# Spread sums of attention by two matmuls with ones, and two banks for keys, in a two-layer hybrid kernel on one Trainium2 core

## The chip, the cores and the metric

The kernel runs on one core of a Trainium2 chip (trn2). The metric is the time of one execution on the device in microseconds (us), lower is better. Before the change three runs gave a median of 2713.94 us, 2713.19 to 2719.81.

## What is computed

All data is float32. The input x is (4, 128, 64, 64): 4 batches of 4096 tokens with 128 channels. Two layers follow one another.

```python
# layer 0: group norm, full softmax attention over 4096 tokens of a batch
h = group_norm(x, norm_w, norm_b)            # 32 groups
q, k, v = h @ Wq + bq, h @ Wk + bk, h @ Wv + bv
attn = softmax(q @ k.T * C ** -0.5)          # 4096 x 4096 for each batch
x = x + (attn @ v) @ Wo + bo
# layer 1, on tokens t = (4, 4096, 128)
kv = silu(norm(t) @ W_kv.T)                  # 8 heads, k and v of 128 each
s = q_proj . k;  e = exp(s - cummax(s))
t = t + mean over heads of cumsum(e * v) / cumsum(e)
p = softmax(norm(t) @ router_w + router_b)   # 8 experts, the 2 best kept
t = t + sum over the 2 best of p_e * (norm(t) @ expert_w[e] + expert_b[e])
```

## The kernel before

Every engine has its own program, written out by hand; semaphores tie them together, and each engine runs strictly in the order written. Names below are those of the code, L numbers are lines of the profiled kernel.

**First stage** (`softmax_attention`). A block is 512 queries of a batch: 4 batches of 8 blocks, 32 blocks, numbered n (i = n % 8 inside its batch). A block meets its batch's 4096 keys in 32 tiles of 128 keys; g counts the 1024 tiles and t = g % 32. In the turn of tile g, PE (TensorE) issues three score matmuls (L374 to L376, high and low parts of keys and queries), one matmul that looks for row maxima a block ahead (L359), and three that weigh the values of tile g - 3 (L388 to L390). ACT takes the exponential (`exps`, L500) and its rounded high part (`high`, L505), POOL (GpSimd) the low part (`low`, L224), DVE (VectorE) the row maximum (`row_max`, L638) and the running sum of exponentials (`add`, L654). The rings of tiles are 4 deep, the banks of scores and of maxima 2 deep.

The sum left in `den` (128 keys-within-tile x 512 queries) still has to be added over partitions. `denominators(n)` does that on PE in turn `den_slot`, 1 or 2 of the next block, into the bank `pj_ps`; DVE takes the reciprocal a turn later (`inverse`, L663), SP sends it through DRAM and back as rows spread over all partitions, and `finish` (L671, L675) uses it in turn 10. The single bank `pj_ps` also serves the projections of queries (`project_q`, L278, turn 21 or 22), keys (`project_k`, L294, turns 3, 7, ... of block i = 6) and values (`project_v`, L311, turns 8, 12, ... of block i = 7 and turns 0 and 4 of the next block) of the next batch.

```python
for i in range(QT):                                                     # L405
    mm = pe.matmul(pj_ps[:, i:i + 1], den[:, i * C:(i + 1) * C], ones[:, 0:1], start=True, stop=True)
```

**Second stage** (`scan_attention_and_experts`). The unit is 512 tokens of one batch, 32 of them. In step j the kernel works on the keys of unit k = j, the values of unit v = j - 5 and the experts of unit f = j - 11, so that a step holds three units at once for j from 11 to 31; 43 steps in all. Each step has 8 slots h, one for each head. In slot h PE issues the value matmuls of head h (`value`, three, L1143 to L1145), its key matmuls (`key`, three), and one product of an expert (`expert`, L1186), whose 8 products are added in the bank `mo_ps` after a bias (`expert_bias`, L1178). ACT applies Silu to both; DVE multiplies by the weight (`weigh`, L1373) and scans (`scan`, L1381); POOL multiplies tokens by the gate of an expert (`gated`, L1049) and adds up the heads (`add_head`, L1061). DVE adds the experts to the tokens (`output`, L1401) and the heads (`residual`, L1388). `G_LAG`, `X_LAG` say in which slot the first gate product and the first expert product of a unit stand. Four steps make a group (4 batches of the same 512 tokens): step j % 4 = 0 has the scans and the reciprocal of the weights (L1345 to L1366) on DVE, step 1 the router's logits (L1124, L1126), step 2 the choice of the two experts on DVE (L1423 to L1467).

PSUM has 8 banks. The second stage gives three to values (`v_ps`), one to keys (`k_ps`; for j < 5 a bank of values serves as a second one), one each to row sums and to statistics, and two to expert sums (`mo_ps`). In unit 26 and later, half of the gate products are made by DVE (`by_vector`, `FREE` = 26).

## Time and profile before

| | |
|---|---|
| median of 3 runs | 2713.94 us |
| the profiled execution, its own time | 2719.66 us |
| its span, first to last instruction | 2717.9 us |
| PE busy | 2553.1 us (94%) |
| DVE, ACT, POOL busy | 2152.6 (79%), 1840.3 (68%), 2058.7 us (76%) |
| granted TensorE clock, mean | 0.983 |
| DMA engines, mean in the second stage | about 0.5 to 0.6 busy |

The first stage ends near 1831 us, the second takes the rest. A matmul's duration in the records is longer than its turn on the array, since matmuls overlap; the spacing of starts is what counts. A float32 matmul (experts, projections) is recorded as two instructions and a float32r one as one. Idle time of an engine that nobody waits for costs nothing.

### The profile page before, as it was taken

The page shows a single profiled execution, that of the slowest core. Times are in us where ns is not written, and L with a number is a line of the kernel's source. Part 1 is how long each engine was busy: PE and PEld are TensorE (multiplying, and loading weights), DVE is VectorE, ACT ScalarE, POOL GpSimd, SP SyncE. Part 2 cuts the span into 40 slices and gives each one's busy share as a digit, 9 for nine tenths or more (in the row PEclk, how much of TensorE's full clock was granted, in tenths as well). Part 3 has the DMA queues.
Part 4 walks back from the last instruction along what each step waited for, and adds up shares of the span by engine and source line. Part 5 has one row for each costly group of instructions (what it writes and reads, how often), then busy time and mean ns, then how long its engine had stood idle before and what let it go on. Part 6 is the DMA issues. An engine that isn't in the chain of part 4 may idle for free. (4 is left out here: it accounts for less than half of the span.)

```text
span 2717.9 us, 37024 instructions
## 1 busy us (share of the span) xinstructions
PE 2553.1 (94%) x10851; PEld 1856.2 (68%) x10851; DVE 2152.6 (79%) x3225; ACT 1840.3 (68%) x3375; POOL 2058.7 (76%) x1688
## 2 busy tenths in 40 slices
PE   6999999999999999999999999997889999999868
PEld 4888877788887788887778888773545555555433
DVE  6788887788887778888778978852888988888884
ACT  5667677676667766677766766765877777767540
POOL 4777777777776777777677777772558988989994
PEclk9999999999999999999999999998999999999899
DMA  1000000100000010000001000101445565555545
GB/s 66 9 9 9 13 12 9 40 8 13 12 9 9 8 41 15 9 9 12 9 13 32 9 12 13 47 8 53 171 172 218 186 240 214 213 204 196 227 173 198
DMA packets 58105, 198.38 MB, mean 73 GB/s; under 512 B 12752, under 2 KB 15376, under 8 KB 40496
## 3 DMA queue, kind: packets, MB, share of 16 engines
q1 hardware_dynamic: 57904, 196.03, 20.4%
q8 instruction: 86, 1.41, 0.2%
q14 instruction: 115, 0.94, 0.1%
HBM read 178.04 MB, written 17.96 MB: 72 GB/s over the span
## 5 line engine op out<-in xcount | busy, mean ns | idle before, releaser
L224 POOL TENSOR_TENSOR p_lo<-pf,p_hi 128x512 fp32r<-128x512 f32 x1024 | 1320.0, 1292 | 434.2 <-ACT p_hi L505 431.7
L500 ACT ACTIVATE pf<-s_ps 128x512 f32<-128x512 f32 x1024 | 612.8, 598 | 530.4 <-PE s_ps L376 529.3
L638 DVE TENSOR_REDUCE mx<-m_ps 128x1 f32<-128x512 f32 x1024 | 702.2, 687 | 296.1 <-PE m_ps L359 292.2
L654 DVE TENSOR_TENSOR sum_ps<-sum_ps,pf 128x512 f32<-128x512 f32 x960 | 661.6, 689 | 21.1 <-ACT pf L500 20.8
L505 ACT CAST p_hi<-pf 128x512 fp32r<-128x512 f32 x1024 | 627.2, 613 | 0.0
L374 PE MATMUL s_ps<-q_hi,kd_hi 128*128 128x512 f32 x1024 | 427.2, 417 | 0.0
L359 PE MATMUL m_ps<-w_both,q_hi 128*128 128x512 f32 x1024 | 403.6, 395 | 7.0 <-DVE mx L638 6.0
L388 PE MATMUL om_ps<-p_hi,v_hi 128*128 128x512 f32 x1024 | 401.3, 392 | 4.6 <-POOL p_lo L224 4.6
L376 PE MATMUL s_ps<-q_lo,kd_hi 128*128 128x512 f32 x1024 | 399.7, 390 | 0.0
L375 PE MATMUL s_ps<-q_hi,kd_lo 128*128 128x512 f32 x1024 | 399.6, 390 | 0.0
L389 PE MATMUL om_ps<-p_hi,v_lo 128*128 128x512 f32 x1024 | 399.1, 390 | 0.0
L390 PE MATMUL om_ps<-p_lo,v_hi 128*128 128x512 f32 x1024 | 398.8, 389 | 0.0
L1049 POOL TENSOR_TENSOR xg<-gate_b,tv 128x512 f32<-128x512 f32 x232 | 303.8, 1316 | 46.0 <-PE mo_ps L1186 31.9
L1061 POOL TENSOR_TENSOR acc<-acc,ay 128x512 f32<-128x512 f32 x192 | 255.2, 1329 | 61.6 <-DVE ay L1381 56.6
L1186 PE MATMUL mo_ps<-xg,ew 128*128 128x512 f32 x512 | 271.1, 625 | 28.1 <-POOL xg L1049 25.6
L1381 DVE TENSOR_TENSOR_SCAN ay<-ay,carry,v_ps 128x512 f32<-128x512 f32 x224 | 286.7, 1280 | 8.7 <-DVE v_ps L1373 0.3
L1250 ACT ACTIVATE v_ps<-v_ps 128x512 f32<-128x512 f32 x256 | 149.7, 585 | 166.1 <-PE v_ps L1145 164.6
L1373 DVE TENSOR_TENSOR v_ps<-bq,v_ps 128x512 f32<-128x512 f32 x256 | 174.9, 683 | 85.4 <-ACT v_ps L1250 70.2
L359 PEld LDWEIGHTS m_ps<-w_both,q_hi 128*128 128x128 f32 x1024 | 192.4, 188 | 60.1 <-DVE mx L638 17.2
L388 PEld LDWEIGHTS om_ps<-p_hi,v_hi 128*128 128x128 f32 x1024 | 192.1, 188 | 55.5 <-POOL p_lo L224 14.2
L374 PEld LDWEIGHTS s_ps<-q_hi,kd_hi 128*128 128x128 f32 x1024 | 192.7, 188 | 50.5 <-issue 15.1
L375 PEld LDWEIGHTS s_ps<-q_hi,kd_lo 128*128 128x128 f32 x1024 | 192.7, 188 | 48.5 <-issue 12.7
(205 smaller groups left out, 3481.0 us busy)
## 6 DMA issues: line engine op xcount, KB each, us to landing
bq<-weight_rows SPq DMA_DIRECT2D x64, 1024.0 KB, 6.3
gate_b<-gate_rows SPq DMA_DIRECT2D x64, 1024.0 KB, 4.8
xb<-in_x_dram SPq DMA_DIRECT2D x8, 1024.0 KB, 6.2
rb_sb<-inverse_rows SPq DMA_DIRECT2D x32, 256.0 KB, 3.9
tokens<-xb SPq DMA_DIRECT2D x32, 256.0 KB, 2.0
tp<-tokens SPq DMA_DIRECT2D x32, 256.0 KB, 5.4
rb<-norm_rows SPq DMA_DIRECT2D x32, 256.0 KB, 5.4
tv<-tokens SPq DMA_DIRECT2D x32, 256.0 KB, 5.5
```

What stands on the lines that cost most here:

```text
L224: nc.gpsimd.tensor_tensor(p_lo[:, r, :], pf[:, r, :], p_hi[:, r, :].bitcast(F32), ALU.subtract).then_inc(lo_done, 1)
L359: pe.matmul(m_ps[:, j % 2, :], q_hi[:, n % QRING, sub * C:(sub + 1) * C], kp[:, chunk * BANK:(chunk + 1) * BANK], start=True, stop=True).t ...
L374: pe.matmul(dst, kd_hi[:, ks], q_hi[:, q, :], start=False, stop=False, skip_group_check=True)
L375: pe.matmul(dst, kd_lo[:, ks], q_hi[:, q, :], start=False, stop=False, skip_group_check=True)
L376: pe.matmul(dst, kd_hi[:, ks], q_lo[:, q, :], start=False, stop=True, skip_group_check=True).then_inc(s_pe, 1)
L388: pe.matmul(o, v_hi[:, t, :], p_hi[:, r, :], start=(t == 0), stop=False)
L389: pe.matmul(o, v_lo[:, t, :], p_hi[:, r, :], start=False, stop=False)
L390: pe.matmul(o, v_hi[:, t, :], p_lo[:, r, :], start=False, stop=(t == KT - 1)).then_inc(pv_pe, 1)
L500: nc.scalar.activation(pf[:, g % RING, :], s_ps[:, g % 2, :], ACT.Exp, scale=SCALE).then_inc(exp_done, 1)
L505: nc.scalar.copy(p_hi[:, g % RING, :], pf[:, g % RING, :]).then_inc(hi_done, 1)
L638: nc.vector.tensor_reduce(mx[:, n % 2, sub, chunk:chunk + 1], m_ps[:, j % 2, :], AX.X, ALU.max).then_inc(m_max, 1)
L654: nc.vector.tensor_tensor(sum_ps[:], sum_ps[:], p, ALU.add).then_inc(sum_done, 1)
```

## The change

First stage:

- `denominators` of all blocks but the last adds `den` over partitions by two float32r matmuls of 512 columns, with a matrix of ones as the stationary operand and the high and the low part of `den` as moving ones, so that every row of `pj_ps` holds all 512 sums. ACT makes the high part (`high_den`, turn 2), POOL the low part (`low_den`, turn 3); PE's turn is now 5 (6 where i = 0).
- `inverse` (turn 6 or 7) has to bring the sums to partitions: DVE multiplies the bank by the identity, four blocks wide, into `den`, sums each block of 128 (`tensor_reduce`) and takes the reciprocal of the 128 x 4 result.
- What waited for `inv_done` before using `pj_ps` waits for `den_held`, the first of these three. `finish` moves from turn 10 to 14, and the one-time work of blocks 27 and 30 moves a few turns.

Second stage:

- Keys have two banks in all steps, alternating by head; expert sums have one. From unit 27 on, odd units take a bank of values, which are done by then.
- `add_head` of head h moves from slot h + 1 to h + 2, `gated` and `expert` one slot later (`G_LAG` 4, `X_LAG` 6), except that the eighth product of a unit shares the seventh's slot; `output` moves from slot 5 to 4, `residual` from 1 to 2. `logits` moves from slot 3 to 5, what follows it accordingly.
- `expert_bias` of a unit up to 26 waits for `output` of the unit before.

```diff
-        def den_slot(i):
-            return 1 if i == NB - 2 else 2
+        def den_slot(n):
+            return 6 if n % NB == 0 else 5
...
@@ -223,6 +224,10 @@
                 r = g % RING
                 nc.gpsimd.tensor_tensor(p_lo[:, r, :], pf[:, r, :], p_hi[:, r, :].bitcast(F32), ALU.subtract).then_inc(lo_done, 1)
...
+            def low_den(n):
+                pool.wait_ge(den_h, n + 1)
+                nc.gpsimd.tensor_tensor(den_lo[:], den[:], den_hi[:].bitcast(F32), ALU.subtract).then_inc(den_l, 1)
...
             for g in range(TILES + 1):
                 if g >= 1:
                     low(g - 1)
+                if KT <= g < TILES and g % KT == 3:
+                    low_den(g // KT - 1)
...
             def denominators(n):
-                pe.wait_ge(sum_done, (n + 1) * KT)
                 pe.wait_ge(q_l, min(n + 3, BLOCKS))
                 if n % NB == NB - 1 and n + 1 < BLOCKS:
-                    pe.wait_ge(v_l, (n // NB + 1) * CK + 7)
+                    pe.wait_ge(v_l, (n // NB + 2) * CK)
+                elif n % NB == NB - 3 and n // NB + 1 < B:
+                    pe.wait_ge(k_diff, (n // NB + 1) * CK + 1)
                 elif n % NB == NB - 2 and n // NB + 1 < B:
                     pe.wait_ge(k_diff, (n // NB + 2) * CK)
-                after(pe, inv_done, n)
+                after(pe, den_held, n)
                 if n == BLOCKS - 1:
                     pe.wait_ge(wt_lo, 4)
                 if n == L_AT:
                     pe.wait_ge(diff_dve, 1)
-                for i in range(QT):
-                    mm = pe.matmul(pj_ps[:, i:i + 1], den[:, i * C:(i + 1) * C], ones[:, 0:1], start=True, stop=True)
-                mm.then_inc(den_pe, 1)
+                if n < BLOCKS - 1:
+                    pe.wait_ge(den_l, n + 1)
+                    pe.matmul(pj_ps[:], ones_r[:], den_hi[:], start=True, stop=False)
+                    pe.matmul(pj_ps[:], ones_r[:], den_lo[:], start=False, stop=True).then_inc(den_pe, 1)
+                else:
+                    pe.wait_ge(sum_done, (n + 1) * KT)
+                    for i in range(QT):
+                        mm = pe.matmul(pj_ps[:, i:i + 1], den[:, i * C:(i + 1) * C], ones[:, 0:1], start=True, stop=True)
+                    mm.then_inc(den_pe, 1)
...
+            def high_den(n):
+                act.wait_ge(sum_done, (n + 1) * KT)
+                after(act, den_pe, n)
+                nc.scalar.copy(den_hi[:], den[:]).then_inc(den_h, 1)
...
+                    if n and t == 2:
+                        high_den(n - 1)
...
-                    after(dve, den_pe, n)
+                    after(dve, diag_sum, n)
                     nc.vector.tensor_tensor(den[:], sum_ps[:], p, ALU.add).then_inc(sum_done, 1)
 
             def inverse(n):
                 dve.wait_ge(den_pe, n + 1)
                 after(dve, inv_out, 16 * (n - 1))
-                nc.vector.reciprocal(rinv[:, n % 2, :], pj_ps[:, 0:QT]).then_inc(inv_done, 1)
+                if n == BLOCKS - 1:
+                    nc.vector.reciprocal(rinv[:, n % 2, :], pj_ps[:, 0:QT]).then_inc(inv_done, 1)
+                    return
+                blocks = den[:].rearrange("p (i c) -> p i c", i=QT)
+                nc.vector.tensor_tensor(blocks, pj_ps[:].rearrange("p (i c) -> p i c", i=QT),
+                                        ident[:].unsqueeze(1).to_broadcast([C, QT, C]), ALU.mult).then_inc(den_held, 1)
+                dve.wait_ge(den_held, n + 1)
+                nc.vector.tensor_reduce(dsum[:], blocks, AX.X, ALU.add).then_inc(diag_sum, 1)
+                dve.wait_ge(diag_sum, n + 1)
+                nc.vector.reciprocal(rinv[:, n % 2, :], dsum[:]).then_inc(inv_done, 1)
...
-                    if n and t == den_slot(i) + 1:
+                    if n and t == den_slot(n) + 1:
                         inverse(n - 1)
-                    if n and t == 10:
+                    if n and t == 14:
...
-    V_LAG, F_LAG, G_LAG, X_LAG = 5, 11, 3, 5
+    V_LAG, F_LAG, G_LAG, X_LAG, A_LAG = 5, 11, 4, 6, 2
...
         v_ps = psum("v_ps", [C, 3, BANK])
-        k_ps = psum("k_ps", [C, BANK])
+        k_ps = psum("k_ps", [C, 2, BANK])
         row_ps = psum("row_ps", [C, BANK])
-        mo_ps = psum("mo_ps", [C, 2, BANK])
+        mo_ps = psum("mo_ps", [C, BANK])
         st_ps = psum("st_ps", [C, BANK])
...
-        def two_banks(k):
-            return k < V_LAG
...
         def value_bank(v, h):
             return v_ps[:, (v * HEADS + h) % 3, :]
 
         def key_bank(k, h):
-            return v_ps[:, 1, :] if two_banks(k) and h % 2 else k_ps[:]
+            return k_ps[:, h % 2, :]
+
+        def sum_bank(f):
+            return v_ps[:, 0, :] if f > FREE and f % 2 else mo_ps[:]
+
+        def expert_slot(e):
+            return X_LAG + min(e, E - 2)
...
-                    if h == 0 and stage(v - 1):
-                        add_head(v - 1, HEADS - 1)
+                    if h < A_LAG and stage(v - 1):
+                        add_head(v - 1, HEADS + h - A_LAG)
...
-                    if stage(v) and h:
-                        add_head(v, h - 1)
+                    if stage(v) and h >= A_LAG:
+                        add_head(v, h - A_LAG)
...
             def key(k, h):
                 if h == 0:
                     pe.wait_ge(xl_pool, k + 1)
-                after(pe, k_act, k * HEADS + h - (1 if two_banks(k) else 0))
+                after(pe, k_act, k * HEADS + h - 1)
                 project(key_bank(k, h), h, 0, k).then_inc(k_pe, 1)
 
             def value(v, h):
-                if v == 0 and h == 0:
-                    pe.wait_ge(k_act, V_LAG * HEADS)
                 after(pe, y_dve, v * HEADS + h - 2)
                 project(value_bank(v, h), h, 1, v).then_inc(v_pe, 1)
...
             def expert_bias(f):
                 s, b, cols = place(f)
-                after(pe, out_dve, f - 1)
+                if f > FREE and f % 2:
+                    pe.wait_ge(y_dve, NBLK * HEADS)
+                after(pe, out_dve, f - 1 if f > FREE else f)
                 pe.wait_ge(gt_act, s + 1)
-                pe.matmul(mo_ps[:, f % 2, :], eb_hi[:, b, :], gt[:], start=True, stop=False)
-                pe.matmul(mo_ps[:, f % 2, :], eb_lo[:, b, :], gt[:], start=False, stop=False)
+                pe.matmul(sum_bank(f), eb_hi[:, b, :], gt[:], start=True, stop=False)
+                pe.matmul(sum_bank(f), eb_lo[:, b, :], gt[:], start=False, stop=False)
...
-                    if norm2_at(j, 1) is not None and h == 3:
+                    if norm2_at(j, 1) is not None and h == 5:
                         logits(norm2_at(j, 1))
-                    if norm2_at(j, 1) is not None and h == 5:
+                    if norm2_at(j, 1) is not None and h == 6:
                         turn_logits(norm2_at(j, 1))
-                    if stage(f - 1) and h < X_LAG:
-                        expert(f - 1, E + h - X_LAG)
-                    if stage(f) and h >= X_LAG:
-                        if h == X_LAG:
-                            expert_bias(f)
-                        expert(f, h - X_LAG)
+                    if stage(f) and h == X_LAG:
+                        expert_bias(f)
+                    for e in range(E):
+                        if stage(f) and expert_slot(e) == h:
+                            expert(f, e)
+                        if stage(f - 1) and expert_slot(e) == h + HEADS:
+                            expert(f - 1, e)
...
-                    if stage(f - 1) and h == X_LAG:
+                    if stage(f - 1) and h == expert_slot(E - 1) - HEADS:
                         output(f - 1)
...
-                    if stage(v - 1) and h == 1:
+                    if stage(v - 1) and h == 2:
                         residual(v - 1)
```

**Where rows moved.** DVE, first stage, round `inverse` (L663 before, L686 to L691 now; L638 and L657 are `row_max`, L654 and L673 `add`). Before:

```order
L654 TENSOR_TENSOR sum_ps<-sum_ps,pf 128x512 [waits sum_done,exp_done]
L638 TENSOR_REDUCE mx<-m_ps 128x1 [waits m_pe]
L654 TENSOR_TENSOR sum_ps<-sum_ps,pf 128x512 [waits sum_done,exp_done]
L663 RECIPROCAL rinv<-pj_ps 128x4 [waits inv_out,den_pe]
L638 TENSOR_REDUCE mx<-m_ps 128x1 [waits m_pe]
L654 TENSOR_TENSOR sum_ps<-sum_ps,pf 128x512 [waits sum_done,exp_done]
```

Now:

```order
L673 TENSOR_TENSOR sum_ps<-sum_ps,pf 128x512 [waits sum_done,exp_done]
L657 TENSOR_REDUCE mx<-m_ps 128x1 [waits m_pe]
L673 TENSOR_TENSOR sum_ps<-sum_ps,pf 128x512 [waits sum_done,exp_done]
L686 TENSOR_TENSOR den<-pj_ps,ident 128x512 [waits inv_out,den_pe]
L689 TENSOR_REDUCE dsum<-den 128x4 [waits den_held]
L691 RECIPROCAL rinv<-dsum 128x4 [waits diag_sum]
L657 TENSOR_REDUCE mx<-m_ps 128x1 [waits m_pe]
L673 TENSOR_TENSOR sum_ps<-sum_ps,pf 128x512 [waits sum_done,exp_done]
```

One short instruction has become three, and it stands three tiles later in the block.

PE, second stage, slots 3 and 4 of a step: products of experts into `mo_ps`, values into `v_ps`, keys into `k_ps`. Before:

```order
L1186 MATMUL mo_ps<-xg,ew 128x512 [waits xg_pool]
L1143 MATMUL v_ps<-xh,w_both 128x512 [waits y_dve]
L1144 MATMUL v_ps<-xl,w_both 128x512
L1145 MATMUL v_ps<-xh,w_both 128x512
L1143 MATMUL k_ps<-xh,w_both 128x512 [waits k_act]
L1144 MATMUL k_ps<-xl,w_both 128x512
L1145 MATMUL k_ps<-xh,w_both 128x512
L1186 MATMUL mo_ps<-xg,ew 128x512 [waits xg_pool]
```

Now:

```order
L1217 MATMUL mo_ps<-xg,ew 128x512 [waits xg_pool]
L1174 MATMUL v_ps<-xh,w_both 128x512 [waits y_dve]
L1175 MATMUL v_ps<-xl,w_both 128x512
L1176 MATMUL v_ps<-xh,w_both 128x512
L1174 MATMUL k_ps<-xh,w_both 128x512 [waits k_act]
L1175 MATMUL k_ps<-xl,w_both 128x512
L1176 MATMUL k_ps<-xh,w_both 128x512
L1217 MATMUL mo_ps<-xg,ew 128x512 [waits xg_pool] x2
```

In slot 4 two products stand behind each other, the seventh and the eighth of the unit; the bias of the next unit comes in slot 6, where before it came in slot 5.

DVE, second stage, the same step from slot 2 or 3: `tv<-acc,tv` is `residual`, `tv<-mo_ps,tv` is `output`. Before:

```order
L1373 TENSOR_TENSOR v_ps<-bq,v_ps 128x512 [waits v_act,b_in2]
L1381 SCALAR_TENSOR_TENSOR ay<-ay,carry,v_ps 128x512 [waits y_pool,a_act,z_dve]
L1373 TENSOR_TENSOR v_ps<-bq,v_ps 128x512 [waits v_act,b_in0]
L1381 SCALAR_TENSOR_TENSOR ay<-ay,carry,v_ps 128x512 [waits y_pool,a_act,z_dve]
L1401 TENSOR_TENSOR tv<-mo_ps,tv 128x512 [waits x_pe]
L1373 TENSOR_TENSOR v_ps<-bq,v_ps 128x512 [waits v_act,b_in0]
```

Now:

```order
L1420 SCALAR_TENSOR_TENSOR tv<-acc,tv 128x512 [waits tv_in0,y_pool]
L1405 TENSOR_TENSOR v_ps<-bq,v_ps 128x512 [waits v_act,b_in2]
L1413 SCALAR_TENSOR_TENSOR ay<-ay,carry,v_ps 128x512 [waits y_pool,a_act,z_dve]
L1433 TENSOR_TENSOR tv<-mo_ps,tv 128x512 [waits x_pe]
L1405 TENSOR_TENSOR v_ps<-bq,v_ps 128x512 [waits v_act,b_in0]
L1413 SCALAR_TENSOR_TENSOR ay<-ay,carry,v_ps 128x512 [waits y_pool,a_act,z_dve]
```

`output` stands one head earlier than it did, ahead of the first weighing of the second half of the heads (`b_in0`), and `residual` one head later.

## Rows read from the trace of the kernel before

**Rows 1.** Busy time by stretch (us, count), then clock, DMA share, GB/s.

```profile
60.00:1831.00 1771.00, 1749.07 (x7808) 1417.28 (x7806) 1428.23 (x2305) 1243.01 (x2340) 1344.16 (x1044) 1.00 0.05 15
1831.00:2080.20 249.20, 203.80 (x860) 111.17 (x861) 170.90 (x200) 182.11 (x311) 138.65 (x137) 0.92 0.40 142
2080.20:2471.50 391.30, 361.52 (x1450) 206.78 (x1449) 334.02 (x408) 275.48 (x485) 353.37 (x302) 0.98 0.58 210
```

**Rows 2.** Timeline of PE round one block's denominators: start us, us.

```profile
220.69 0.39 PE L388 MATMUL om_ps<-p_hi,v_hi 128*128 128x512 f32 x1
...
221.37 0.95 PE L405 MATMUL pj_ps<-ones,den 128*128 128x1 f32 x8
222.18 0.48 PE L374 MATMUL s_ps<-q_hi,kd_hi 128*128 128x512 f32 x1
222.50 0.39 PE L375 MATMUL s_ps<-q_hi,kd_lo 128*128 128x512 f32 x1
```

**Rows 3.** Timeline, first stage: the low part of one tile and its use.

```profile
224.34 1.29 POOL L224 TENSOR_TENSOR p_lo<-pf,p_hi 128x512 fp32r<-128x512 f32 x1 [1.20 <-ACT p_hi L505]
...
227.94 0.39 PE L388 MATMUL om_ps<-p_hi,v_hi 128*128 128x512 f32 x1
```

**Rows 4.** Timeline of DVE, first stage: a block's finish, then back on time.

```profile
235.69 1.08 DVE L671 TENSOR_TENSOR om_ps<-om_ps,rb_sb 128x512 f32<-128x512 f32 x1
236.81 0.75 DVE L675 SCALAR_TENSOR_TENSOR xb<-om_ps,bvo,xb 128x512 f32<-128x512 f32 x1
...
245.59 0.69 DVE L638 TENSOR_REDUCE mx<-m_ps 128x1 f32<-128x512 f32 x1 [0.26 <-PE m_ps L359]
```

**Rows 5.** Waits of PE, first stage: us in total, times, longest.

```profile
PE om_ps L388 <- POOL p_lo L224: 4.1, 10, 0.5
PE pj_ps L278 <- DVE kd L624: 2.5, 3, 0.8
...
PE m_ps L359 <- DVE mx L638: 0.7, 2, 0.4
```

**Rows 6.** Waits of PE, 2080.2 to 2471.5 us; last row 1831 to 2080.2.

```profile
PE k_ps L1143 <- ACT sk L1246: 19.4, 12, 2.3
PE st_ps L1124 <- ACT sq L1262: 5.6, 3, 2.0
PE v_ps L1143 <- DVE ay L1381: 2.4, 2, 1.2
PE mo_ps L1186 <- POOL xg L1049: 1.7, 4, 0.4
...
PE k_ps L1143 <- ACT sk L1246: 19.5, 15, 3.5
```

**Rows 7.** Timeline of PE and of ACT round one wait, second stage.

```profile
2296.75 0.39 PE L1145 MATMUL v_ps<-xh,w_both 128*128 128x512 f32 x1
2299.39 0.50 PE L1143 MATMUL k_ps<-xh,w_both 128*128 128x512 f32 x1 [2.25 <-ACT sk L1246]
...
2293.21 1.28 ACT L1317 ACT_TABLE_LOAD   x1
...
2296.35 1.28 ACT L1322 ACT_TABLE_LOAD   x1
...
2298.75 0.59 ACT L1246 ACTIVATE sk<-k_ps 128x512 f32<-128x512 f32 x1
```

**Rows 8.** Timeline of DVE in a step with row sums, second stage.

```profile
2353.48 1.26 DVE L1356 TENSOR_TENSOR_SCAN u_r<-e_r,u_r,zeros 128x512 f32<-128x512 f32 x1
2354.78 3.35 DVE L1362 RECIPROCAL b_r<-u_r 128x512 f32<-128x512 f32 x1
```

**Rows 9.** Timeline of PE after the last values: logits, then their transposes.

```profile
2650.95 1.52 PE L1124 MATMUL st_ps<-tv,rwz 128*32 128x512 f32 x8
...
2653.26 1.98 PE L1186 MATMUL mo_ps<-xg,ew 128*128 128x512 f32 x4
2655.08 0.60 PE L1132 MATMUL st_ps<-ident,l_sb 128*128 128x128 f32 x4
```

More of the change, by code:

```diff
@@ L85, in softmax_attention @@
         nmax = sb("nmax", [C, 2, QT])
-        den = sb("den", [C, QB])
+        den, dsum = sb("den", [C, QB]), sb("dsum", [C, QT])
+        wv, wo, wvT = (den[:, i * C:(i + 1) * C] for i in range(3))
+        den_hi, den_lo = sb("den_hi", [C, QB], F32R), sb("den_lo", [C, QB], F32R)
         rinv = sb("rinv", [C, 2, QT])
@@ L265, in project_q @@
                 else:
-                    after(pe, inv_done, n - 2)
+                    after(pe, den_held, n - 2)
                 if n >= 2 and n % NB == 0:
@@ L327, in center_experts @@
                 if g == 0:
[L328 removed]
+                    pe.wait_ge(den_held, E_AT)
                 else:
@@ L1308, in _ @@
                         square_of_mean(norm1_at(j, 0))
-                    if norm2_at(j, 1) is not None and h in (1, 2):
-                        for b in (2 * h - 2, 2 * h - 1):
+                    if norm2_at(j, 1) is not None and h in (3, 4):
+                        for b in (2 * h - 6, 2 * h - 5):
                             square_out(norm2_at(j, 1), b)
-                    if norm2_at(j, 1) is not None and h == 4:
+                    if norm2_at(j, 1) is not None and h == 5:
                         hold_logits(norm2_at(j, 1))
```

46 lines of the change are left out of this document (21 added, 25 removed).

## The prediction

> **What bounds the kernel now.** I read the busy time by stretch first [rows 1]. In the first stage, 60 to 1831 us, PE is busy 1749.07 of 1771.00 us, DVE 1428, POOL 1344 and ACT 1243: PE sets the time there, and whatever leaves PE's queue leaves the total, as long as nobody makes PE wait. In the second stage, from 2080.2 to 2471.5 us, the work repeats in groups of four steps, four of them in 391.3 us, 97.8 us each. PE's records cover 361.5 us, POOL's 353.4, DVE's 334.0. None is alone the bound: here PE waits, and the question is what for.
>
> The timeline of PE [rows 2] gives prices. Three float32r matmuls take 220.69 to 221.37, so 0.227 us each. The waits of PE in the first stage [rows 5] are small: 4.1 us on POOL's low parts, 2.5 us on a key chunk, 0.7 us on row maxima. In the second stage [rows 6] PE waits 29.1 us in the four groups, 7.3 us each, and 19.4 of them are a key matmul that waits for ACT to empty the single key bank. One such wait is shown [rows 7]: ACT loads a table, works, and loads another, 2293.21 to 2297.6, so the next Silu of a key starts at 2298.75, and PE stands from about 2297.1 to 2299.39. Without waits a group would take PE 97.8 - 7.3 = 90.5 us; POOL's 353.4 / 4 = 88.4 us is close behind, DVE's 83.5 less so.
>
> **First stage, removed and added on PE.** The old denominators are eight records from 221.37; the second matmul behind them, L375, starts at 222.50. Taking off one ordinary spacing, they cost 222.50 - 221.37 - 0.227 = 0.90 us [rows 2]. The new ones are two float32r matmuls of 512 columns, 2 x 0.227 = 0.45 us. 31 blocks change: 31 x 0.45 = **13.9 us less**.
>
> The Trainium skill, page TensorE: Matmul & The Clock Gate, section Back-to-back issue gap, gives a matmul of 1 to 64 columns about 60 cycles, some 25 ns at full clock. By that the eight cost an estimated 0.2 us, and the change would lose 0.25 us a block, 8 us in all. The trace disagrees: their turns are 0.81 / 8 = 0.1 us each (221.37 to 222.18), and the matmul behind them comes late as well. The sum goes by the trace.
>
> **What the other engines get.** ACT gains one copy of 128x512 in a block (nearest: 0.59 us of a Silu, [rows 7]), POOL one subtraction (1.29 us), DVE a multiplication and a reduction. For the cover of POOL: the low part of tile 3 ends at 224.34 + 1.29 = 225.63 and PE wants it at 227.94 [rows 3], 2.3 us later, so 1.29 us of extra work in turn 3 is hidden, and POOL wins back 7 x 0.227 - 1.29 = 0.3 us in every tile. In the block with i = 0 a low part of keys stands one turn ahead, and the two together reach 2.3 us; if this is late, PE waits about 0.5 us as in the ten cases of [rows 5], three times. For DVE: the multiplication reads a bank and the identity and is nearest to a 512-wide operation of 0.69 us or, being four blocks wide, to the 1.08 us of `finish` [rows 4]; the reduction is nearest to the 0.69 us of L638. Together 1.4 to 1.8 us at once. `finish` puts 1.8 us (235.69 to 237.48) on DVE in one go, which waits for PE again at 245.59, and PE waited for row maxima only 0.7 us in the whole stage. So I cost this at nothing; if the cover were gone, the wait that [rows 5] shows, up to 0.4 us, would come in 31 blocks, 12 us. Round trip of the inverses: `inverse` is four turns later and so is `finish`, nothing changes.
>
> **Added waits on `pj_ps`.** In block i = 6 a key chunk now stands two turns before the denominators (3 and 5), and these wait for DVE to finish its difference. The same distance, chunk in turn 19 and query projection in turn 21, costs PE 2.5 us in three batches today [rows 5]; I add 2.5 us. What is queued behind is the whole of PE. The next key chunk, and once the first weight transposes, stand two turns behind the denominators and wait for DVE's multiplication. DVE reaches it about a turn later; between nothing and 1 us at four places, I take 0.3 each, 1.2 us. The value chunks of block i = 0 keep their distance of two turns.
>
> First stage: -13.9 + 2.5 + 1.2 = **-10 us**, bounds -14 (no wait anywhere) and about 0 (the 12 us of DVE added in part).
>
> **Second stage, the second key bank.** In the case of [rows 7] PE would go on with the waiting key matmuls (0.7 us), a product (0.91 us: four records from 2653.26 to 2655.08 are two products [rows 9]) and the next value (0.7 us), until about 2299.4, when the Silu of 2298.75 is done. The wait of 2.25 us goes nearly whole. So most of the 19.4 us could go. But PE then meets the next limit. DVE is the slow one in the steps with row sums, where a scan and a reciprocal stand 1.26 + 3.35 us in its queue [rows 8]; values have three banks only, and POOL's 88.4 us is only 2 us under PE's 90.5. I take half of the 7.3 us as won, a group of 94.1 us. The 20 steps with keys, values and experts together (j = 12 to 31) are five groups: 5 x 3.7 = **-18.5 us**. Bounds: all of it, -37; none, 0. Before that, 1831 to 2080.2, PE waits 19.5 us for ACT [rows 6], but its busy share there is low ([rows 1], 203.80 of 249.2 us) and DVE and the start-up of the pipeline set the pace; I take -3.
>
> **The later slots.** POOL adds heads one slot later, which removes waits of POOL on DVE, and the squares of the logits are asked for later, which should spare part of PE's 5.6 us [rows 6]; both are inside the half. The eighth product now stands one slot behind its gate product where it had two; POOL lags most in the quiet steps, and this is why I don't take more than half. At the end, logits come behind the last two products, where these used to stand between logits and transposes: 1.8 us of products (2653.26 to 2655.08) no longer hide ACT's copy, and the residual waits one gate product longer. Nothing covers this, the end of the kernel hangs on the gates of the last group: **+2.5 us**, between 0 and 5.
>
> Second stage: -18.5 - 3 + 2.5 = **-19 us**. Together -29 us: the profiled execution of 2719.66 would be 2690.7. It is 5.7 us above the median of the runs, 2713.94, and from that the same difference gives **2685 us**.
>
> **Rival 1, the waits only move.** PE's waits in the second stage become waits for values on DVE or for gate products on POOL, since their busy times are within 8% of each other [rows 1]. Against it: the waits of PE on these two are 2.4 and 1.7 us today. Then only the first stage counts: 2713.9 - 10 = 2704.
>
> **Rival 2, the single bank of expert sums makes it slower.** The bias of unit f waits for `output` of f - 1, and `output` now stands before the weighing of head 4 and waits for the eighth product, which is behind a key and another product in PE's queue: some 0.7 + 1.8 us of waiting on DVE in each step, with four weighings and scans queued behind it; in the step with row sums the 4.6 us of [rows 8] stand ahead of `output` too, and PE's bias arrives 1.4 us after scan 3, so it would wait up to 3.9 us. If DVE's loss comes through at 1.5 us a step in 26 steps: +39 - 10, 2743 us. It decides for slower from 0.4 us net a step on (10 / 26). Against it: PE needs the scan of head 4 only for value 7, and has a value, two keys, row sums, bias and product to do meanwhile; today PE waits for DVE only 2.4 us in four groups [rows 6]. The Trainium skill, page Perfetto Trace Analysis, section Matmuls, says that independent matmul groups should rotate through different banks, so that the emptying of one overlaps the next. The change does this for keys and undoes it for expert sums; no row of before shows the single bank.
>
> **Rival 3, the whole gain.** All PE waits of the groups go, and the first stage adds none: -14 - 37 - 3 = 2660 us. For it speaks that ACT's table loads are the cause of most of the waits; against it POOL's 88.4 us.
>
> **Numbers.** Forecast (2670 to 2700) 0.58, rival 1 0.24, rival 3 0.11, rival 2 0.07. The range 2663 to 2707 holds the forecast, rival 1 and half of rival 3. 0.3% is 8.1 us, about what a measurement can tell, so the border is 2705.8: rival 1 lies six parts in ten under it, and a little of it above 2722. Faster 0.83, same 0.09, slower 0.08.
>
> **What the next profile would show.** The end of the first stage near 1821 instead of 1831 us; the spacing round the denominators 0.45 us and an ordinary block 0.45 us shorter; PE waiting for POOL's low parts and for row maxima no more than today; a new wait of denominators on the key difference, near 0.8 us, three times. In the second stage: waits of key matmuls on Silu near zero, a group of steps of about 94 us, PE's waits on values or on POOL grown to 3 us a group. Wrong would be: a group at 97 or more with waits on DVE in PE's list (rival 1), a bias that waits for `output` in most steps (rival 2), or a first stage that has not shrunk because row maxima come late.

## The result, and the profile after

The changed kernel takes 2700.22 us (median of 7 runs, 2697.51 to 2707.79) where the kernel before takes 2718.55 on the same chip. The ratio, formed from the means (2702.11 and 2717.64), is 0.9943, with an interval of 0.9927 to 0.9959: 15.5 us less, of the 29 forecast (the medians differ by 18.3). In all the runs of this document three executions took far longer than the others of their kernel, 2912.7, 4222.4 and 7775.6 us, and the ratios leave them out. The profiled execution took 2707.49 us with a span of 2705.7, against 2719.66 and 2717.9: 12.2 us less. By place:

| stretch of the span | before | after | difference | forecast |
|---|---|---|---|---|
| to the last denominators | 1830.60 | 1825.29 | -5.3 | -10 |
| from there to the last residual | 816.48 | 803.44 | -13.0 | -21.5 |
| from there to the last output | 67.5 | 73.6 | +6.1 | +2.5 |

Busy time by stretch, changed kernel (columns as in [rows 1]):

```profile
60.00:1826.00 1766.00, 1741.50 (x7639) 1401.37 (x7637) 1462.30 (x2369) 1259.08 (x2372) 1382.21 (x1077) 1.00 0.05 15
1826.00:2075.90 249.90, 202.82 (x867) 114.93 (x866) 172.47 (x203) 181.49 (x315) 139.22 (x137) 0.91 0.39 142
2075.90:2460.50 384.60, 356.80 (x1453) 205.63 (x1452) 338.63 (x407) 274.18 (x485) 355.50 (x304) 1.00 0.57 215
```

Four groups of steps, counted from the residual that opens the first, now take 384.6 us instead of 391.3, 96.2 each instead of 97.8; 94.1 were forecast. VectorE is busy 4.6 us longer in a stretch 6.7 us shorter, though it does the same work. Waits of PE in these four groups, after:

```profile
PE v_ps L1174 <- DVE ay L1413: 11.6, 15, 1.2
PE mo_ps L1209 <- DVE tv L1433: 9.2, 4, 3.0
PE st_ps L1169 <- DVE g L1499: 7.0, 4, 1.8
```

The key's wait for its Silu, 19.4 us in [rows 6], is gone, and the list is nearly as long as before: 27.8 us, all of it on VectorE, where before it was 29.6 (the 29.1 of the prediction and 0.5 at the gates). L1209 is the bias product into the single bank of expert sums, L1169 the turn of the gates. The chain of waits of the changed kernel says what stands behind the bias wait (start, length, place):

```profile
2244.97 2.35 DVE u_r L1388
...
2247.52 3.10 issue
2250.62 0.64 DVE tv L1433
...
2251.30 0.50 PE mo_ps L1209
2251.80 0.23 PE mo_ps L1210
2252.03 1.31 PE mo_ps L1217 x2
```

The 3.10 us called issue are the reciprocal, which holds VectorE's queue. So PE waits for `output`, which stands behind the sums and reciprocal of the rows. This recurs at 2148.59, 2244.97, 2342.22 and 2438.61, once a group. And the sums have become slower: 2.33 us, where [rows 8] show 1.26. The timeline of POOL and DVE shows what goes with it. Changed kernel:

```profile
2244.94 1.30 POOL L1092 TENSOR_TENSOR acc<-acc,ay 128x512 f32<-128x512 f32 x1
2246.19 2.22 POOL L1080 TENSOR_TENSOR xg<-gate_b,tv 128x512 f32<-128x512 f32 x1
...
2244.97 2.34 DVE L1388 TENSOR_TENSOR_SCAN u_r<-e_r,u_r,zeros 128x512 f32<-128x512 f32 x1
2247.35 3.35 DVE L1394 RECIPROCAL b_r<-u_r 128x512 f32<-128x512 f32 x1
```

Kernel before, POOL beside the scan of [rows 8]:

```profile
2353.54 2.29 POOL L1061 TENSOR_TENSOR acc<-acc,ay 128x512 f32<-128x512 f32 x1
```

Before, the scan starts 0.06 us ahead of POOL's addition: the scan takes 1.26 us and the addition 2.29 instead of 1.28. Now the addition starts 0.03 us ahead, the scan takes 2.34, and the gate product behind the addition takes 2.22 instead of 1.28. It is so in all four groups of either trace. The Trainium skill, page SBUF — State Buffer, section Who interferes with whom, says that a VectorE instruction with two SBUF inputs contends with a GpSimd instruction that reads SBUF, that the ports which the two engines share are an exclusive lock, and that the order of issue decides who blocks. These traces agree.

The lags of the change are not needed for this, and the added microsecond need not be its price. The kernel that has the change in its first stage alone runs the second stage of before, instruction for instruction, and shows:

```profile
2247.54 2.42 DVE L1384 TENSOR_TENSOR_SCAN u_r<-e_r,u_r,zeros 128x512 f32<-128x512 f32 x1
2247.61 1.27 POOL L1089 TENSOR_TENSOR acc<-acc,ay 128x512 f32<-128x512 f32 x1
2248.84 2.20 POOL L1077 TENSOR_TENSOR xg<-gate_b,tv 128x512 f32<-128x512 f32 x1
```

Its scan takes 2.38 to 2.42 us in all four groups, although the record of the scan starts up to 0.07 us ahead of the addition's, so starts so close together in the records don't tell who comes first. And its groups take 97.85 us, where the kernel before, with scans of 1.26, has 97.8. In that order of instructions, where PE doesn't wait for `output` at the bias, the longer scan cost nothing that can be seen. What it costs in the changed kernel no run isolates.

A small instruction of the gates' chain grows too. Before, then after (shortest, median, longest, ns):

```profile
L1449 DVE TENSOR_TENSOR gap<-top x4: 148/149/150, 2112.6 to 2407.8; 128x16 f32<-128x16 f32 x4
```

```profile
L1481 DVE TENSOR_TENSOR gap<-top x4: 1259/1267/1269, 2102.7 to 2392.7; 128x16 f32<-128x16 f32 x4
```

The timeline shows what stands beside it in the changed kernel:

```profile
2102.14 0.67 DVE L1420 SCALAR_TENSOR_TENSOR tv<-acc,tv 128x512 f32<-128x512 f32 x1
2102.30 1.66 POOL L1092 TENSOR_TENSOR acc<-acc,ay 128x512 f32<-128x512 f32 x1 [1.23 <-DVE ay L1413]
2102.72 1.27 DVE L1481 TENSOR_TENSOR gap<-top 128x16 f32<-128x16 f32 x1
```

`residual`, which the change put in this slot, now stands between the scan and this subtraction, so that POOL's addition, which waits for the same scan, starts 0.42 us ahead of the subtraction. Before, the subtraction came right behind the scan and 0.16 us ahead of the addition (2112.64 and 2112.80). With the second stage of before it takes 0.15 us in every group; in every run with this `residual` it takes 1.2 us or more in these groups. It stands ahead of `g`, for which PE waits 7.0 us in four groups at L1169 (0.5 before).

In the first stage, PE round the new denominators, then its waits (60 to 1826 us):

```profile
227.43 0.39 PE L395 MATMUL om_ps<-p_lo,v_hi 128*128 128x512 f32 x1
227.66 0.46 PE L412 MATMUL pj_ps<-den_hi,ones_r 128*128 128x512 f32 x1
227.96 0.40 PE L413 MATMUL pj_ps<-den_lo,ones_r 128*128 128x512 f32 x1
228.19 0.40 PE L379 MATMUL s_ps<-q_hi,kd_hi 128*128 128x512 f32 x1
```

```profile
PE om_ps L393 <- POOL p_lo L225: 5.6, 13, 0.5
...
PE pj_ps L285 <- DVE kd L643: 2.6, 3, 0.9
PE pj_ps L412 <- issue: 2.4, 3, 0.8
...
PE m_ps L364 <- DVE mx L657: 1.3, 3, 0.5
PE pj_ps L412 <- POOL den_lo L229: 0.4, 1, 0.4
```

The two new matmuls take 228.19 - 227.66 = 0.53 us, not 0.45: the first has a spacing of 0.30. An ordinary block fell from 53.09 to 52.73 us, by 0.36. The trace calls the releaser of three waits at L412 `issue`; in the code they are for the key difference (DVE's L643, which ends 0.11 us before the matmul at 389.79).

### The profile page after: what moved, and what is told of

The parts are those of the page before. It is cut to its first block and busy times, and to the rows that moved or that the text cites. A ratio compares the mean times of both kernels' runs of the same rounds, so it can differ in the third digit from the quotient of the medians.

```text
span 2705.7 us, 36807 instructions
## 1 busy us (share of the span) xinstructions
PE 2539.7 (94%) x10665; PEld 1841.5 (68%) x10665; DVE 2194.0 (81%) x3287; ACT 1851.4 (68%) x3406; POOL 2095.1 (77%) x1719
## 5 line engine op out<-in xcount | busy, mean ns | idle before, releaser
L657 DVE TENSOR_REDUCE mx<-m_ps 128x1 f32<-128x512 f32 x1024 | 701.0, 686 | 256.7 <-PE m_ps L364 249.8
L673 DVE TENSOR_TENSOR sum_ps<-sum_ps,pf 128x512 f32<-128x512 f32 x960 | 661.5, 689 | 20.0 <-ACT pf L512 19.5
L1217 PE MATMUL mo_ps<-xg,ew 128*128 128x512 f32 x464 | 242.9, 622 | 20.8 <-POOL xg L1080 18.0
```

The costliest lines, as they stand in the source:

```text
L657: nc.vector.tensor_reduce(mx[:, n % 2, sub, chunk:chunk + 1], m_ps[:, j % 2, :], AX.X, ALU.max).then_inc(m_max, 1)
L673: nc.vector.tensor_tensor(sum_ps[:], sum_ps[:], p, ALU.add).then_inc(sum_done, 1)
```

## The experiments

Ratios are against the kernel before, from 5 rounds each (3 for the single wait); the changed kernel has 0.9943. A difference of 0.001 is 2.7 us, and an interval is about 0.0013 wide to either side.

**The stages apart.** One kernel has the change in the first stage alone, one in the second alone.

> The change's first stage with the second stage of before. Theory (the first stage gave about 7 us, the body of the second about 13, and the tail took 6 back): 6 to 8 us under before, ratio near 0.9972; ordinary blocks of 52.73 us. Rival (the first stage's own term of 10 us holds and the profile of the change had a slow start): 10 us, ratio 0.9963. Second rival (the first stage gave nothing in the total, as its end is hidden by the start of the second): ratio 1.000.

> The change's second stage with the first stage of before. Theory: 7 to 9 us under before (13 from the steps, 6 lost after the last value), ratio near 0.997; the groups of four steps 96.2 us against 97.8. Rival (the two parts don't add, the second stage alone gives the whole 15): ratio 0.9943.

Measured: 0.9973 (0.9960 to 0.9985) and 0.9979 (0.9970 to 0.9988), some 7.3 and 5.7 us. Together 13, near the 15.5: within the noise the parts add. The groups take 97.85 and 96.4 us.

**The banks back**, with the lags kept.

```diff
-        k_ps = psum("k_ps", [C, 2, BANK])
-        mo_ps = psum("mo_ps", [C, BANK])
+        k_ps = psum("k_ps", [C, BANK])
+        mo_ps = psum("mo_ps", [C, 2, BANK])
```

> The changed kernel with one bank for keys and two for expert sums, as before, all its later slots kept. Theory (the second key bank pays 4 to 5 us a group in waits on Silu, and the single sum bank costs 2.3 us a group back): key waits on Silu return at some 19 us in four groups, the bias no longer waits for output, groups of 98 to 99 us, and the total is 8 to 12 us over the change. Rival (the gain of the second stage is from the later slots of POOL, not from the banks): groups stay at 96.2 us or fall to 94, total equal or lower than the change.

Measured: 0.9989 (0.9980 to 0.9997), groups of 98.1 us: the theory. The wait of keys is back, that of the bias gone:

```profile
PE k_ps L1174 <- ACT sk L1278: 21.5, 11, 2.3
```

With the lags in place the banks are worth 0.0046, 12 us. Against the first stage alone (0.9973) the lags without the banks cost 0.0016, 4 us, which the intervals don't separate from nothing.

**The burst of sums and reciprocal, moved.** One head later, and one head earlier (with ACT's exponential):

```diff
-                        if h == 3:
+                        if h == 4:
                             sums(s)
                             inverse(s)
-                        if h == 4:
+                        if h == 5:
                             new_weights(s)
```

> The changed kernel with the row sums' scan and reciprocal one slot later on DVE (slot 4 instead of 3, behind output and the scan of head 4), and the new weights one slot later. Theory (PE's bias waits for output because 4.6 us of scan and reciprocal stand ahead of it, 2.3 us in each group): the wait of mo_ps L1209 on output goes from 9.2 us in four groups to under 1, groups of about 94 us, 10 to 15 us less in all. Rival (DVE is the bound in that step and the wait only moves to PE's value matmuls): PE's waits on scans grow by the same 2 us a group and the total stays within 3 us. A third case: the weights' rows go out about 2 us later and ACT and DVE wait longer for bq, slower by a few us.

> The second-stage softmax of the gates one head earlier: ScalarE's exponential of the rows at h = 1, VectorE's sums and reciprocal at h = 2, its new weights at h = 3 (in the changed kernel 2, 3 and 4). Theory A (the gain of the second stage was given back at the chain reciprocal, new weights, row DMA, next group's gate products): the wait of the bias product on the output (9.2 us in four) and the waits for the landed rows (ScalarE 13.9 us in four, VectorE 6.1) fall to under 3 us together, a group of four steps takes 94 us instead of 96.2, and the time is 8 to 12 us under the changed kernel's. Theory B (VectorE's own work is the bound once the Silu wait is gone, so the reciprocal costs its time wherever it stands): the same waits come back as waits of the value products on VectorE, the groups stay within 0.5 us of 96, and the time within 2 us.

Measured: 0.9986 (0.9977 to 0.9995) and 0.9977 (0.9966 to 0.9989), both slower than where it stands. Later, the weights' rows land late: in the groups ACT waits 18.1 us for them and DVE 10.1 (13.9 and 6.1 in the changed kernel), and PE 20.3 for the values. Earlier, the bias wait is gone and PE stands at a value (one such row, then the sum in the groups):

```profile
2256.68 0.50 PE L1174 MATMUL v_ps<-xh,w_both 128*128 128x512 f32 x1 [3.52 <-DVE ay L1413]
```

```profile
PE v_ps L1174 <- DVE ay L1413: 24.7, 16, 3.5
```

Groups of 97.8 us on average. Neither theory of the second run holds in full: the waits moved, as B says, but grew, from 27.8 to 31.7 us. No wait of ACT or DVE for the weights' rows is left in the trace's list, and the groups are longer all the same, so the late rows are not what holds them up.

**The output ahead of the burst.**

```diff
-                    if stage(f - 1) and h == expert_slot(E - 1) - HEADS:
+                    if stage(f - 1) and h == expert_slot(E - 1) - HEADS and rows_at(j) is None:
                         output(f - 1)
...
                         if h == 3:
+                            if stage(f - 1):
+                                output(f - 1)
                             sums(s)
```

> In the steps with a softmax of the rows, VectorE writes the output of the expert sums at the end of h = 3, ahead of the sums and the reciprocal, instead of at h = 4 behind them. Theory A (TensorE's wait at the bias product, 9.2 us in four, is the price of the single bank of expert sums whose reader stands behind the 5 to 6 us of sums and reciprocal): the wait goes to near zero, a group of four steps falls from about 96.2 to about 94, the time 8 to 12 us under the changed kernel's. Theory B (the burst costs TensorE its time wherever it stands, as in the run with the softmax one head earlier, where the wait came back at the value products): the bias wait goes, the waits of the value products rise by as much, time within 2 us.

Measured: 0.9947 (0.9935 to 0.9959), no change; groups of 95.7 us. The bias wait of 9.2 us is gone and the values' has grown by 7.9, from 11.6. Theory B:

```profile
PE v_ps L1174 <- DVE ay L1413: 19.5, 16, 3.1
```

**Three quarters of the reciprocal left out.** Leaves out 384 of 512 columns of the reciprocal, in all groups but the first.

```diff
-                nc.vector.reciprocal(b_r[:], u_r[:]).then_inc(ri_dve, 1)
+                n = C if s else TOK
+                nc.vector.reciprocal(b_r[:, :n], u_r[:, :n]).then_inc(ri_dve, 1)
```

> Leaves out three quarters of the reciprocal of the rows' sums (128 of 512 columns, in all groups but the first), so that VectorE's burst of sums and reciprocal falls from 5.7 to about 3.2 us. Theory A (this burst is what TensorE waits for, in whatever wait it shows): the bias wait falls from 9.2 us in four to under 1, the wait for landed rows on ScalarE (13.9) and VectorE (6.1) by 2 us a group, groups from 96.2 to about 94, the time 10 us or more under the changed kernel's. Theory B (TensorE's waits are spread over all of VectorE's and GpSimd's work): the bias wait goes and half of it or more comes back at the value products, the time under 4 us less.

Measured: 0.9893 (0.9879 to 0.9906), 13.6 us under the changed kernel. Theory A. The instruction fell by 2.40 us, and the bias wait is all but gone:

```profile
L1395 DVE RECIPROCAL b_r<-u_r x4: 953/954/954, 2141.4 to 2423.6; 128x128 f32<-128x128 f32 x4
```

```profile
PE mo_ps L1209 <- DVE tv L1434: 0.6, 1, 0.6
```

Seven times 2.40 is 16.8; groups took 93.5 us on average instead of 96.2. The reciprocal is on the path of the changed kernel with its whole length, although VectorE is busy only 88% of the stretch. That the scan beside it counts in the same way is likely, but no run shows it.

**The reciprocal in two halves**, 256 columns at h = 3 and 256 at the end of h = 4.

```diff
-                            inverse(s)
+                            inverse(s, 0)
                         if h == 4:
+                            inverse(s, 1)
                             new_weights(s)
```

> The reciprocal of the rows' sums in two halves of 256 columns: the first behind the sums at h = 3, the second at the end of h = 4 ahead of the new weights, so that VectorE's work stays and its burst falls from 5.7 to about 4 us; the output at h = 4 stands behind half a reciprocal only. Theory A (it costs as a burst, since VectorE is idle 28 us in 385 beside it waiting for ScalarE): half of what the quarter reciprocal gave, groups about 95, the time 4 to 8 us under the changed kernel's. Theory B (it costs as total work, VectorE being what the values wait for all through the group): groups stay at 96, time within 2 us.

Measured: 0.9952 (0.9938 to 0.9966), no gain, theory B. The halves take 1.74 us each, 0.13 more in all, and PE waits 19.4 us for values and 2.9 at the bias. The groups take 97.0 us. So VectorE's work in the row steps counts, not the length of one burst.

**The gates turned one head later.**

```diff
-                    if norm2_at(j, 2) is not None and h == 6:
+                    if norm2_at(j, 2) is not None and h == (7 if norm2_at(j, 2) < SUPERS - 1 else 6):
                         turn_gates(norm2_at(j, 2))
...
```

> The turn of the gate rows (the small transposing products and the hold of their result) at h = 7 instead of 6, in all groups but the last. In the changed kernel TensorE waits there 7.0 us in four for VectorE's last gate factor. Theory A (this wait is on the path): it goes to near zero, a group is about 1.5 us shorter, the time 5 to 9 us under the changed kernel's. Theory B (TensorE would wait for the values or for the output right after it anyway): the wait goes and the value waits rise by as much, time within 2 us.

Measured: 0.9924 (0.9911 to 0.9936), 5 us less than the changed kernel, though the two intervals overlap; groups of 94.9 us. The wait of 7.0 us is gone, 4.7 us came back at the values, and 2.6 left the bias. The scan of the row sums fell from 2.33 to 1.80 us as well, so the 5 us are not those of the gates' wait alone.

```profile
PE v_ps L1174 <- DVE ay L1413: 16.3, 22, 1.2
...
PE mo_ps L1209 <- DVE tv L1433: 6.6, 4, 2.4
```

**The lags.** Additions with no lag, with one head of lag, and products one head earlier:

```diff
-    V_LAG, F_LAG, G_LAG, X_LAG, A_LAG = 5, 11, 4, 6, 2
+    V_LAG, F_LAG, G_LAG, X_LAG, A_LAG = 5, 11, 4, 6, 0
```

> Of the change's three lags only GpSimd's additions go back: each head is added in its own step of the loop (A_LAG 0 instead of 2); banks, products and experts stay as changed. Theory A (the later additions are what frees GpSimd from waiting for VectorE's scans, so that the gate products come in time): GpSimd waits for the scans again, TensorE waits for the gate products, groups of four steps take 98 or more, the time 8 to 12 us over the changed kernel's, though the tail is some 2 us shorter. Theory B (GpSimd is busy 92% of the stage and only its order changes): groups stay at 96, and the time is 1 to 3 us less by the shorter tail.

> GpSimd's additions one head behind the scans (A_LAG 1), as in the kernel before, all else as changed. Theory A (the second head of lag matters: the last two products share a slot, and their gate products must not stand behind an addition that waits for VectorE): TensorE waits for the gate products some 5 us in four groups, groups 97 to 98, the time 3 to 8 us over the changed kernel's. Theory B (one head of lag was enough): groups stay at 96, the stretch after the last residual 1 to 2 us shorter, the time the same or up to 2 us less.

> Only the lags of the gate products and of the experts go back (G_LAG 3 and X_LAG 5 instead of 4 and 6); two key banks, one bank of expert sums and the later additions stay. The output then stands at h = 3, ahead of sums and reciprocal. Theory A (the place of the output against the reciprocal decides): the bias wait of 9.2 us in four goes, groups about 94, time 6 to 12 us under the changed kernel's. Theory B (with the additions two heads later, products one head earlier come too early for GpSimd and for the residual two heads behind): TensorE waits for the gate products, 3 us a group or more, groups 97 or more, time over the changed kernel's.

The first was misnamed: the kernel before adds one head behind, so 0 goes one step past it. It takes 1.0144 (1.0129 to 1.0158), 55 us over the changed kernel, far more than either theory said: POOL waits 47.7 us in the groups for a scan with a gate product queued behind, and PE for that product:

```profile
PE mo_ps L1217 <- POOL xg L1080: 34.0, 27, 3.1
```

With one head of lag the time is that of the changed kernel, 0.9945 (0.9932 to 0.9957), theory B, with groups of 95.1 us. In them 4.8 us of waits for gate products have come, and the bias wait has fallen from 9.2 to 1.6. The earlier products give 0.9957 (0.9945 to 0.9969) and groups of 96.3 us: the bias wait goes (theory A), the value waits grow from 11.6 to 16.7 us, no gain.

**The first product with one wait instead of three**, in ordinary blocks (the wait that stays is the one for the low part).

```diff
-                pe.wait_ge(q_l, min(n + 3, BLOCKS))
+                plain = n % NB < NB - 3 and n < BLOCKS - 6
+                if not plain:
+                    pe.wait_ge(q_l, min(n + 3, BLOCKS))
...
-                after(pe, den_held, n)
+                if not plain:
+                    after(pe, den_held, n)
```

> In the first stage's ordinary blocks the new denominators' product waits for one semaphore (the exponentials) instead of three. Theory A (the first new product's 0.30 us against 0.23 of the next ones is the price of handling three waits): its spacing becomes 0.23, a block 52.66 instead of 52.73 us, all of it 1.5 to 2 us less. Theory B (the 0.30 us belongs to the product itself, the change of operand or weights behind the float32 products): it stays 0.30 and the time the same.

Measured: the spacing is 0.23 and a block 52.69 us (52.66 expected), theory A in the trace; the ratio is 0.9943 (0.9929 to 0.9957), too small a gain to be seen there.

```profile
227.13 0.39 PE L415 MATMUL pj_ps<-den_hi,ones_r 128*128 128x512 f32 x1
227.36 0.39 PE L416 MATMUL pj_ps<-den_lo,ones_r 128*128 128x512 f32 x1
227.59 0.39 PE L379 MATMUL s_ps<-q_hi,kd_hi 128*128 128x512 f32 x1
```

**The tail in a shorter order**: last additions first, last logits at h = 4, the gate factors ahead of the output.

> Only the end of the second stage changes: GpSimd adds the last two heads of the last unit first, the logits of the last group stand one head earlier (h = 4), and the factors of gate row 4 stand before the output there. Theory A (the lag of the additions lengthens the serial tail): the stretch from the last residual to the last output falls from 73.6 to about 69 us (before: 67.5), the time 4 to 5 us under the changed kernel's. Theory B (the tail is set by the chain of the gates' own reciprocal and row DMA, and by a lower granted clock there): the stretch stays over 72 us, time within 2 us.

Measured: 73.6 falls to 70.2 us, between the theories; ratio 0.9933 (0.9921 to 0.9946), not told from 0.9943. But the run with one wait, whose code there is that of the changed kernel, took 67.3. Between two outputs each, changed kernel and then that run (the figure behind the counts is the granted clock):

```profile
2659.20:2673.30 14.10, 10.13 (x19) 4.19 (x18) 3.74 (x6) 0.00 (x0) 6.78 (x5) 0.76 0.61 199
...
2682.00:2693.70 11.70, 9.32 (x19) 3.84 (x18) 3.78 (x6) 0.00 (x0) 6.79 (x5) 0.85 0.56 204
```

```profile
2655.60:2666.00 10.40, 7.54 (x19) 3.13 (x18) 4.04 (x5) 0.00 (x0) 6.12 (x5) 1.00 0.74 258
...
2675.60:2684.30 8.70, 7.89 (x19) 3.09 (x19) 4.90 (x5) 0.00 (x0) 4.78 (x5) 1.00 0.77 271
```

PE is busy with the same 19 matmuls for 10.13 or 7.54 us, and the stretches last 14.1 or 10.4. Of the 3.7 us between them 2.6 are PE's own; 1.1 are its wait for the first gate product of that unit, 3.97 us in the slow case and 2.86 in the fast one.

**Together.** Output ahead, gates later, one wait and tail; then halves in place of output ahead; then one head of lag, gates later, one wait and early last logits:

> Four edits together: output ahead of the reciprocal, gate rows turned at h = 7, the tail's shorter order, and one wait for the new denominators' product. Theory A (they act in different places and add): the changed kernel's time less 8 to 12 (output), 4 (gate rows), 1 to 3 (tail) and 1 (wait), some 2683. Theory B (VectorE binds once the two waits are gone): no better than the gate rows' edit alone, some 2695.

> The reciprocal in two halves, with the gate rows turned at h = 7, one wait for the new denominators' product, and the tail's shorter order. Theory A: under the four-edit run by 2 to 6 us, some 2689. Theory B: the same as the four-edit run, 2693.

> Gate rows turned at h = 7, one wait for the new denominators' product, the last logits at h = 4, and the additions one head behind. Theory A of adds_one: over the four-edit run's time by some 5 us, near 2698. Theory B of adds_one: the tail's part comes in full, some 2692.

Measured: 2693.26 us, 0.9917 (0.9904 to 0.9930); 2695.14 us, 0.9908 (0.9894 to 0.9922); 2698.97 us, 0.9932 (0.9919 to 0.9946). The first two can't be told apart. They are ahead of the changed kernel by 7 to 10 us (the second with an interval clear of its own), and of the kernel before by 23 to 25. The gates' edit alone has 0.9924: theory B of the first, in substance. The third can't be told from the changed kernel.

## Why the forecast was half right

**The step that failed** is the size of the term for the second key bank, "a group of 94.1 us, 5 x 3.7 = -18.5 us". The mechanism was right: the wait of keys on Silu, 19.4 us, went to nothing, and the banks are worth 12 us. The five groups gave 8.1 us together, 1.6 each, where 3.7 were forecast. The group behind them, without keys, gave 5.8 us (82.6 to 76.8) for which the sum had no term. The sum took half of PE's waits as won because VectorE's scan and reciprocal, 1.26 + 3.35 us, would be the next limit. The limit was named rightly and priced wrongly: with 2.40 us of reciprocal less, a group was 2.6 us shorter. What is left on the path costs its whole length, so a share of the old waits is no measure. The waits that took the place of the keys' were on VectorE: 11.6 us for values, 9.2 for the bias and 7.0 for the gates in four groups. A better sum would have followed PE and VectorE through one step with row sums. That the median, 2700.22 us, still lies inside the range of 2663 to 2707 is owed to the width of the range, which was to hold rival 1 as well.

**What the sum left out** is that VectorE's instructions can grow beside POOL's. In the changed kernel the scan takes 1.07 us more in each group and the small operation before the gates 1.12. The second goes with the new slot of `residual`. The first needs none of the change's lags, since it comes with the second stage of before too, and there it didn't lengthen the groups; its share in the missing 2.1 us of a group is open. The sum had no term for POOL and VectorE meeting, though the profile of before showed it beside the scan: an addition of 2.29 us where others take 1.28. Nor had it one for the turn of the gates, where PE now waits 1.75 us in each group.

**The stretch 1831 to 2080.** -3 was taken; from the last denominators to the residual that opens the groups, 249.6 became 250.6. The key waits fell there from 19.5 to 8.6 us, and waits for values rose from 2.9 to 16.8.

**First stage, -10.** Forecast -13.9 for matmuls; measured 31 x 0.36 = 11.2. The old price was right (0.53 + 0.36 = 0.89 against 0.90), the new one was 0.08 short: three waits on the first product. The wait for the key difference is as forecast, 2.4 us in three. Waits at four places on VectorE's multiplication were forecast at 1.2 and are not in the list. Nothing was put down for POOL's low parts and for row maxima: +1.5 and +0.6. Gone are 0.9 and 1.8 us of waits (L257, and L405 on a value part). The list also has 0.4 us at the first new product, on the low part of `den`. In sum -11.2 + 2.4 + 1.5 + 0.6 + 0.4 - 0.9 - 1.8 = -9.0. The trace shows -5.3, of which 2.2 us were lost in the first 60 us, where four matmuls from 19.2 us took 3.62 us instead of 2.40 and the granted clock from 24 to 60 us was 0.91 instead of 0.95; both differ from one execution to the next (the four matmuls took 2.47 to 3.62 us in other runs, and 3.14, at a clock of 0.91, in the one with the first stage of before). Over all executions the stage ends at 1830.6 and 1831.8 without this part of the change and at 1823.1 to 1825.4 with it, 6 to 7 us. A rest of 2 us was not found.

**Tail, +2.5.** +6.1 in the profiled execution, but 67.3 us, none, in another with the same code. Two profiles with the old order show 67.5 and 68.4 us, both at a mean granted clock of 0.91. Of ten with the changed order eight lie at 70.9 to 73.6 us and a clock of 0.89 to 0.91, two at 66.3 and 67.3 us and 0.96. So at the same clock, 0.91 (70.9, 71.7 and 71.8 us), the changed order takes some 3 us more, near the forecast, and the rest goes with the clock. Whether the changed order brings the low clock more often is open.

**Rival 1** (waits only move) was half of the truth in the second stage: 27.8 us of waits took the place of 29.6, but the groups got shorter all the same, and the clock of the stretch rose from 0.98 to 1.00. **Rival 2** named the right place: the bias waits for `output`, but only in the step with row sums, 2.3 us once a group instead of every step, and moving it gains nothing. **Rival 3** is excluded by the waits on VectorE, which came in place of those on ACT and are the whole list after the change.

## What to carry to other kernels

When a change takes away the wait that ends last, price the next limit by its whole length, by following one period of the loop with the banks counted, and not by a share of the waits. When a change shifts two engines against each other, look for instructions whose duration already varies between two values: they show who blocks whom, and a shift of 0.1 us can swap the roles. But find out in a second run whether the longer duration is on the path before blaming it. A wait that disappears at one place proves little; see whether the period got shorter.

## What was not expected of the hardware

- VectorE and GpSimd hold each other up, and which of them pays can change between two kernels with the same second stage: a scan of 512 columns took 1.26 us beside an addition of 2.29 us, or 2.33 to 2.42 us beside one of 1.28. The records' starts were 0.06 us apart in the first case and from 0.07 us ahead to 0.07 us behind in the second. A 16-column subtraction took 0.15 or 1.27 us.
- A matmul that waited for three semaphores, all long given, had a spacing of 0.30 us; for one, 0.23.
- The granted clock in the last 60 us differs between executions of the same instructions: 0.76 and 1.00 over the same 19 matmuls, which kept PE busy for 10.13 and 7.54 us.
